# Storing later images' rows from GpSimd, scores two steps behind, and picking two experts' rows by products

## The reference

```python
x = x + mixer(_ln_c(x));  t = t + ffn(_ln_t(t))
# block 0: attention over neighbours (12 heads, dilations 1, 2, 3), then one expert of 3 per image
# block 1: Fourier mixer, then 2 experts of 8 per token with a capacity
# block 2: full attention, 12 heads of 16, relative positions, then 2 experts of 8 per token:
probs = softmax(xs @ Wg);  topv, topi = top_k(probs, 2);  cw = topv / sum(topv)
h = relu(dispatched @ W1[e] + b1[e]);  y = h @ W2[e] + b2[e]      # dispatched: tokens sorted by expert
combined = einsum('ks,ksm->sm', cw, rerouted)
# block 3: full attention as in block 2, then one expert of 3 per image
```

## Time and profile before

| | us |
|---|---|
| median of three runs | 855.84 |
| lowest and highest run | 851.66, 859.10 |
| the profiled execution | 851.86 |
| its span, first to last instruction | 850.2 |
| TensorE busy | 666.7 |
| VectorE busy | 376.5 |
| ACT busy | 302.4 |
| GpSimd busy | 202.7 |

### The profile page before, as it was taken

How to read it: one execution, slowest core, us unless ns; L and a number is a source line. 1 busy time by engine, 2 the same in 40 slices (tenths; PEclk the granted TensorE clock), 3 DMA queues, 4 the chain that set the end, 5 groups by cost and what they waited for, 6 DMA issues and landing times. The chain is left out here.

```text
span 850.2 us, 12727 instructions
## 1 busy us (share of the span) xinstructions
PE 666.7 (78%) x3982; PEld 554.7 (65%) x3982; DVE 376.5 (44%) x955; ACT 302.4 (36%) x600; POOL 202.7 (24%) x218
## 2 busy tenths in 40 slices
PE   4896755997996999939986981099995797799297
PEld 2574634695794999925665771099995366577286
DVE  4564645214445244334664745034431466575401
ACT  2343424232312444414343541044452243345222
POOL 5153440001100244421122402523344202231000
PEclk9987987698996999968898985589998689899699
DMA  3736510544106366324765304437762349660342
GB/s 100 188 94 162 140 32 22 124 118 108 31 1 167 103 160 156 52 49 114 197 168 144 93 8 135 148 89 172 184 145 32 79 148 212 169 139 2 83 111 86
DMA packets 96067, 94.93 MB, mean 112 GB/s; under 512 B 17441, under 2 KB 84020, under 8 KB 96008
## 3 DMA queue, kind: packets, MB, share of 16 engines
q1 hardware_dynamic: 85224, 80.25, 35.6%
q0 software_dynamic: 9120, 12.87, 8.6%
q10 hardware_dynamic: 1680, 1.28, 0.6%
HBM read 66.74 MB, written 27.84 MB: 111 GB/s over the span
## 5 line engine op out<-in xcount | busy, mean ns | idle before, releaser
L1925 POOL DMA_INDIRECT sum_scratch<-area,f_row_index x48 | 72.2, 1504 | 189.0 <-DVE area L1876 179.2
L843 DVE TENSOR_REDUCE neg_max<-psum 128x4 f32<-128x1024 f32 x72 | 88.0, 1222 | 65.8 <-PE psum L739 65.5
L921 POOL TENSOR_TENSOR shift<-ident,neg_max 128x256 fp32r<-128x256 f32 x96 | 69.4, 732 | 142.7 <-DVE neg_max L843 85.2
L1651 PE MATMUL psum<-w,area 128*112 128x192 f32 (+1 forms) x576 | 96.2, 326 | 0.0
L1651 PEld LDWEIGHTS psum<-w,area 128*112 128x112 f32 (+1 forms) x576 | 93.4, 183 | 0.0
L751 PE MATMUL psum<-q_parts,k_parts 128*128 128x256 f32 x288 | 84.3, 321 | 5.3 <-POOL shift L921 5.3
L739 PE MATMUL psum<-k_parts,q_parts 128*128 128x256 f32 x288 | 54.4, 316 | 37.4 <-DMA k_parts<-k_scratch 28.8
L752 PE MATMUL psum<-shift,ones_r 128*128 128x256 f32 x288 | 77.3, 297 | 0.0
L751 PEld LDWEIGHTS psum<-q_parts,k_parts 128*128 128x128 f32 x288 | 59.5, 207 | 23.3 <-issue 15.7
L739 PEld LDWEIGHTS psum<-k_parts,q_parts 128*128 128x128 f32 x288 | 43.3, 209 | 44.8 <-issue 31.2
L1745 DVE TENSOR_TENSOR q_parts<-w,q_parts 128x1536 fp32r<-128x1536 f32 x16 | 28.1, 1758 | 90.7 <-ACT q_parts L1676 90.7
(11 more groups left out here) (230 smaller groups left out, 1250.5 us busy)
## 6 DMA issues: line engine op xcount, KB each, us to landing
w<-in_f_w_dram SPq DMA_DIRECT2D x32, 576.0 KB, 4.6
w<-in_f_w_dram SPq DMA_DIRECT2D x16, 384.0 KB, 5.2
w<-in_f_w_dram SPq DMA_DIRECT2D x32, 192.0 KB, 5.8
q_parts<-q_scratch SPq DMA_DIRECT2D x32, 192.0 KB, 3.4
q_scratch<-area SPq DMA_DIRECT2D x22, 192.0 KB, 2.2
q_scratch<-area SPq DMA_DIRECT2D x44, 96.0 KB, 1.9
k_parts<-k_scratch SPq DMA_DIRECT2D x63, 64.0 KB, 3.1
q_parts<-q_scratch SPq DMA_DIRECT2D x32, 96.0 KB, 2.6
```

Of the source, the lines that this page charges most:

```text
L843: ins = dve.tensor_reduce(most, ps[:, 0:2, :].rearrange("p b (c k) -> p (b c) k", c=2), AX_X, ALU.max, negate=True)
L921: ins = nc.gpsimd.tensor_tensor(*shift_of(n, s, b))
L1651: ins = pe.matmul(ps[0:R, 6 + c // 2, D * (c % 2):D * (c % 2 + 1)], x.hidden[:, fc, R * c:R * (c + 1)], net.w2[:, b, fc, :], start=(fc == ...
L1925: pool.indirect_dma_start(net.sum_dram[:, :], bass.IndirectOffsetOnAxis(ap=row_index[0:size, b, c:c + 1], axis=0), x.y[0:size, b, c, :], N ...
```

## The change

In all three attentions the rows of images 2 and 3 are stored by another queue. `rest` lists the stores of an image. GpSimd issues two of them in each step of images 0 (for image 2) and 1 (for image 3), which are now both written out ahead of its loop; in the later two attentions the first six of 16 stay on SP, for image 2 ahead of `load_image(1)` and for image 3 between its pieces. In the first attention the tables go in fours behind pieces 1 and 3 of each image. Also in the first attention only, scores and exponentials run two steps behind (`behind = 2`), scores stand ahead of the quad's products, `finish` takes place at even steps and `store_heads` at odd ones. In f2 the rows of experts 0 and 1 aren't read back for the products: `pick_rows` multiplies the tokens, split into high and low parts by `Norm` ahead of the block, with a 128 x 384 matrix per tile of tokens that marks the slot of each token (`mark_slots`, three buffers), 32 products for an expert. The sorted rows are still stored and loaded, for the weights of all experts and the rows of experts 2 to 7. `rounds` is worked out ahead of the places, and `know_rows` stands ahead of `results` (in f1 too).

```diff
     def all_steps(eng, step, peeled=1):
...
+    behind = 2 if m.local else 1
+    rest = [(kind, half, part) for kind in (*range(kinds), KEY) for half in range(2) for part in range(2)]
+    rest_of_sync = 0 if m.local else 6
+    rest_per_step = 2
...
+            def load_image(i, between=()):
                 for piece, (first, last) in enumerate(PIECES):
                     sp.wait_ge(scored, i * HEADS + (last - HEADS))
                     load_queries(sp, i, piece)
                     load_keys(sp, i, piece)
+                    if piece % 2 == 1:
+                        for kind, half, part in between[piece // 2::2]:
+                            store(sp, kind, half, part, 3, 4, sync_written[3])
+                        if prep:
+                            start_loads(net, sp, itertools.islice(later_tables, 4), prep.loaded)
...
+            for kind, half, part in rest[0:rest_of_sync]:
+                store(sp, kind, half, part, 2, 3, sync_written[2])
+            load_image(1, rest[0:rest_of_sync])
             for i in (2, 3):
-                for kind in (*range(kinds), KEY):
-                    for half in range(2):
-                        for part in range(2):
-                            store(sp, kind, half, part, i, i + 1, rest_written[i])
-                load_image(i - 1)
-                if prep:
-                    start_loads(net, sp, prep.third[i - 2::2], prep.loaded)
-                sp.wait_ge(rest_written[i], DMA * 2 * (of_keys + 2))
-            load_image(IMGS - 1)
+                need(sp, sync_written[i], DMA * rest_of_sync)
+                sp.wait_ge(rest_written[i], DMA * (len(rest) - rest_of_sync))
+                load_image(i)
+            if prep:
+                start_loads(net, sp, later_tables, prep.loaded)
...
+                scores = not peeled or s >= behind
+                if scores and behind == 2:
+                    score(i * PAIRS + (s - behind), (s - behind) % PAIRS)
...
+                if behind == 2 and s % 2 == 0 and not isinstance(i, int):
+                    finish(i - 1, s // 2)
...
+            def store_rest(i, s):
+                at = rest_of_sync + rest_per_step * s
+                for kind, half, part in rest[at:at + rest_per_step]:
+                    store(pool, kind, half, part, i, i + 1, rest_written[i])
+
             def step(i, s):
                 shift(i, s)
                 if isinstance(i, int):
+                    store_rest(i + 2, s)
+                if isinstance(i, int) and i == 0:
                     return
                 if s in (1, 3):
                     stage_v(i, s // 2)
-                if m.local and s % 2 == 0:
+                if m.local and s % 2 == 1:
                     store_heads(i - 1, s // 2)
...
+            pool.wait_ge(high_sb, len(units))
+            pool.wait_ge(low_sb, len(units))
+            for _ in all_steps(pool, step, 2):
...
+    def split_high(self, act, q):
+        act.copy(net.experts.high[:, tiles, :], net.x_norm[:, tiles, 0:D]).then_inc(self.tokens_high, 1)
+    def split_low(self, dve, q):
+        dve.tensor_tensor(net.experts.low[:, tiles, :], net.x_norm[:, tiles, 0:D], net.experts.high[:, tiles, :], ALU.subtract)
...
+            def pick_rows(r, e):
+                for t in range(TILES):
+                    pe.wait_ge(slots_marked, START + (r * PICKED_BY_PRODUCT + e) * TILES + (t + 1))
+                    for k, size in enumerate((P, D2)):
+                        for n, part in enumerate((x.high, x.low)):
+                            ins = pe.matmul(ps[0:size, k, 0:used], part[:, t, P * k:P * k + size], x.is_slot[t % 3],
+                                            start=(t == 0 and n == 0), stop=(t == TILES - 1 and n == 1))
+                    ins.then_inc(slots_used if t < TILES - 1 else turned, 1)
...
-                if turn_next:
+                if turn_next and isinstance(e, int) and e + 1 < PICKED_BY_PRODUCT:
+                    pick_rows(r, e + 1)
+                elif turn_next:
                     turn_rows(r, e + 1, 1 - b)
...
+                step(dve.tensor_tensor(K, A, B, ALU.add))
+                step(dve.scalar_tensor_tensor(out=K, in0=counts[0], scalar=float(slots), in1=K, op0=ALU.add, op1=ALU.mult))
+
+            def mark_slots(r, e):
+                dve.wait_ge(turned, START + job(r, e))
+                for t in range(TILES):
+                    if t >= 3:
+                        dve.wait_ge(slots_used, (r * PICKED_BY_PRODUCT + e) * (TILES - 1) + (t - 2))
+                    dve.tensor_scalar(x.is_slot[t % 3], gate.places[:, 0, :], kept[:, t, e:e + 1], None,
+                                      ALU.is_equal).then_inc(slots_marked, 1)
...
                 def next_and_this(e, b):
                     low_w1(r, e + 1, 1 - b)
                     low_rows(r, e + 1)
+                    know_rows(r, e, b)
                     results(r, e, b)
-                    know_rows(r, e + 1, 1 - b)
 
                 if capacity is None:
+                    mark_slots(r, 0)
                     low_w1(r, 0, 0)
                     low_rows(r, 0)
-                know_rows(r, 0, 0)
+                    for e in range(1, PICKED_BY_PRODUCT):
+                        mark_slots(r, e)
```

96 lines of the change are left out of this document (66 added, 30 removed).

## The result

The changed kernel took 815.21 us in the median of four runs (812.35 to 818.29), the kernel before 853.82 beside it; the ratio is 0.954, with a 95% interval of 0.947 to 0.961. The forecast was 803, its range 792 to 822, 95% for faster. The median of one more measurement of the same kernel was 811.25 (ratio 0.948, 0.944 to 0.952). So the sign and the range held, and the likeliest value was 8 to 12 us too low.

The account below looks back on a forecast made before the run. No engine was taken to bound the whole; the chain is a string of stages, each with its own bound. Gains of 14.5 + 12.1 + 9.5 + 13.8 = 49.9 us from 851.86 gave 802.0, put at 803.0; range 792 to 822.

Parts of the forecast that it names:

- Part 1: First attention's image turns: SP's issuing without the stores about even with the steps; 1.5 us of lateness (0 to 4).
- Part 2: First attention, scores two steps behind: waits for POOL vanish, 2.37 us a step, 17.0 us go from 57.28.
- Rival (e): First attention: two steps behind brings nothing, 2.48 to 2.59 us a step, 806 us; counted inside the forecast's 59%.
- small term for image 0: First attention's image 0: six steps also lose the wait for the shift, about 1 us more gained.
- Part 3: POOL as new store queue: 0.55 us a store, lateness charged 1.0 us in the first attention, 0.8 in each later one.
- (c): Rival: POOL becomes the bound at 1.0 us a store, 5 + 4 + 4 us less gain, 815 us; 8%.
- (d): Rival: slower through 56 stores on POOL, at 1.8 us a store or more; about 868 us at 2.2; 3%.
- Part 4: Second and third attention: time lost at image turns goes, gaining 12.1 and 9.5 us.
- rival (a): Attentions: loads stay late through landing times, store traffic only moved; half the turns' loss stays, 822 us; 15%.
- Part 5: Second expert block: experts 0 and 1 get rows by products instead of waiting for sorted rows, gaining 13.8 us.
- picks of expert 1 5.7: Second expert block: the products that pick expert 1's rows take 5.7 us.
- rival (b): Second expert block: 16 marks delay POOL's stores by 7 us, picks all at low clock; 3 to 6 less, 808; 15%.

Follow-up runs that it names:

- e1: Changed kernel with all 30 table loads of the first attention behind image 3's loads on SP's queue; 810.65 us, ratio 0.951.
- e9: Changed kernel with 18 of 30 table loads at the start of the first attention's block, 12 behind image 3's loads; 813.92 us, ratio 0.954.
- e11: Changed kernel with 10 of 30 table loads behind the first layer norm's own loads, 20 behind image 3's loads; 807.33 us, ratio 0.946.
- e4: Changed kernel with all stores of images 2 and 3 back on SP's queue, tables in halves, as in the kernel before; 847.67 us, ratio 0.993.
- e2: Changed kernel with the first attention's scores, exponentials and finished quads one step behind instead of two; 810.93 us, ratio 0.950.
- e8: Changed kernel with the edits of e1 and e2 together: tables last and one step behind; 811.71 us, ratio 0.949.
- e5: Changed kernel measured once more, nothing edited, as base for the runs beside it; 811.25 us, ratio 0.948.
- e7: Changed kernel with GpSimd's 16 indirect stores of the second expert block begun only after TensorE picked expert 1's rows; 833.12 us (one run).
- e6: Changed kernel with five buffers of marks instead of three; 813.69 us, ratio 0.951.
- e10: e9 plus idle-time TensorE products of 128 columns in the second expert block, 60 ahead of the first picks and 32 behind; 828.65 us, ratio 0.971.
- e12: e11 plus idle-time TensorE products of 256 columns in the second expert block, 26 ahead of the first picks and 14 behind; 808.10 us, ratio 0.946.

## Why the prediction was right, and where it was off

**Part 1, SP's lateness: too small by 3 to 4 us, and the wrong allowance.** The step that failed is "It is about even ... so I add 1.5 us of lateness". The issue times were right (pieces of three in 1.25 to 1.37 us, tables 0.28 to 0.49), and so was the sum of SP's work per image, which leaves no slack. I charged it as if a queue with no slack lost little. The turns came to 45.8 us in place of the 42.8 of the sum. e1, e9 and e11 show that without the tables between pieces the turns take 41.1, within 0.8 of the 40.3 for 17 intervals at 2.37; with them 45.8 to 46.5.

**Part 2, two behind: step length right, its price left out.** An undisturbed pair takes 4.70 to 4.83 us, 2.35 to 2.42 a step. But a piece of `q_parts` and `k_parts` can be loaded only when its heads have been scored, and scoring a step later hands the loads a step (2.35 us) less before the look that needs them. I did not put that in the sum. The four corners show it: one behind 45.1 with and without the tables, two behind 45.8 to 46.5 with and 41.1 without; and with the stores on SP as well (e4) 61.05 against 57.28. That this lost step is the mechanism is argued from the order of the program; that the two edits depend on each other is shown. Rival (e), two behind brings nothing, is what the changed kernel in fact did, but not by the rival's way: it had the steps at 2.48 to 2.59 us, and they took 2.35 to 2.42. That its price, 3 us, was about the size of the miss in this stretch is luck. The small term for image 0 held: from the first maximum to (1,0) it takes 14.95 us, 15.89 before, though all of it began 0.5 later.

**The tail.** Charged 1.0 for the extra score, and that was right: from the last maximum to the last head store it takes 8.17 us before and 9.13 in the changed kernel, and with one behind 8.2 to 8.3 (e2, e8). In the changed kernel the tail grew by 2.5, in e5 by 4.3, and the rest lies behind that store. From there to the reload of the heads it takes 4.5 us before and in e4, where no table stands behind the last loads and SP has the stores, and 5.8 in all the others but e1 (8.9) and e8 (7.1), which have 30 tables there. Which of the two makes the 1.3 us no run separates; from 10 to 20 tables it does not grow. The reload with the products behind it takes 9.3 us before, 9.5 in the changed kernel and up to 11.3 in e5.

**Part 3, GpSimd.** 0.52 to 0.54 us a store against the 0.55 taken; the scores' wait for GpSimd is 0.4 us. Rivals (c) and (d) needed 1.0 and 1.8 us a store and are out.

**Part 4.** 12.1 and 8.4 us against 12.1 and 9.5; over the profiles with stores on GpSimd the means are 10.8 and 9.6. e4 loses them again, which refutes rival (a), that the loads stay late by their landing times: the same transfers, only issued elsewhere, give 54 to 58 us or 66.5 to 67.6.

**Part 5.** Gain 11.5 in the first profile and 10.2 in the mean of the eight that leave this block as it is (209.9), against 13.8. Counted from attention 2's last maximum, expert 0 began at 46.9 us where the sum had 48.9 (66.6 before): the first mark came 1.4 us sooner than forecast and the picks took 7.1 against 8.2 (7.1 to 8.5 in the others, at 0.32 us a product of the low clock and not 0.356), and TensorE then stood 2.2 us, as in the sum (3.1 in e5 and 4.0 in e9, where ACT's copy of the picked rows already came late). From expert 0 to expert 1 it was 21.6 us where the sum had 18.0. So the miss of 1.6 to expert 1's start is 3.6 less 2.0, and the 2.0 hid a part of it. The term that failed is "picks of expert 1 5.7": 9.0 us, and 6.7 to 10.7 in the other profiles. The size of the work was right, as e7 shows (5.58); what was missing is that VectorE and ACT start late behind TensorE beside GpSimd's 16 stores. I had looked at this pair of engines for the reverse, rival (b), marks that delay the stores. A mark lengthened a store by at most 0.2 us (1.14 to 1.16 for 0.97). The long `tensor_tensor` of 1.75 us is another matter, here in the changed kernel:

```profile
511.31 1.75 DVE L1821 TENSOR_TENSOR q_parts<-w,q_parts 128x1536 fp32r<-128x1536 f32 x1
511.44 2.46 POOL L2028 DMA_INDIRECT sorted_scratch<-x_norm,f_to_row  x1 [0.31 <-issue]
```

The store ends 0.84 us after the step does. In the earlier trace rows it is 0.85 us (a store of 1.42, begun 1.19 us into the step). So it is in all twelve profiles in which a store began 0.09 to 1.29 us into such a step: it ends 0.83 to 0.85 us after it. A store that began from 0.3 us ahead to 0.01 us behind the step's start took 0.97 to 0.99 as ever. By these rows the issue of a store that begins inside the step is held until the step ends. The rule weighed in the prediction (the Trainium skill, SBUF — State Buffer, Who interferes with whom) lets `tensor_scalar` lock GpSimd out for its whole length in one of its modes; the marks did not. That they ran in such a mode no row shows: they took 0.42 us for 384 columns, 1.1 ns each, as the `tensor_tensor` did. Of `tensor_tensor` with both inputs in SBUF the same section says that it contends with GpSimd's reads, and infers that it leaves descriptor writing alone; the rows show an indirect store held all the same.

**Sum.** Of the 10.9 us between 49.9 and 39.0, 5.1 lie in the first attention, 2.3 in the picks, 1.1 in attention 3, and 2.7 in a stretch that no edit touches and that no other profile repeats; the rest gave back 0.3.

## What to carry over

When a queue has about as much work as time, read for each item in it what waits for it, and move the items that nobody waits for to where the queue is empty and the transfers too; e11 did that with 10 of 30 loads, and its profile has the gain in all three stretches, while 18 of them a few microseconds later (e9) or all at the end (e1) moved a large part of the loss elsewhere. A change that works a step further behind takes, by the reading of Part 2, that step from whatever refills its buffers; count it together with the queue that does the refilling. And a hand-over between two engines that is free by itself can cost 1.4 us or more beside a run of indirect stores: keep short ping-pong chains (mark, four products, mark) out of their time.

## What the runs showed of the hardware that was not expected

- Beside a run of 16 indirect stores from GpSimd (one each 1.27 us) VectorE and ACT start late behind the TensorE products that they wait for, by 5.0 us in e6 and by 8.5 at the most (the eighth mark of e10, at 527.04 behind products that began at 517.57 to 518.20). It begins 8.5 to 9.2 us after the first store where something waits then (e7, e5), and in e7 it moved with the stores, from the marks to the relus. The cause is open.
- An indirect store whose issue begins 0.09 us or more into VectorE's 128x1536 `tensor_tensor` of 1.75 us ends 0.83 to 0.85 us after that step (12 profiles), so that it takes 1.36 to 2.51 us for 0.97.
- A float32r product of 128 columns took 0.213 us at 1.2 GHz (e10), twice what the 0.32 us for 384 columns gives by proportion.
- In e10 the granted clock (0.50, 1.2 GHz) did not rise in the 13 us of these products, though TensorE was busy 5.00 of 5.00 us; in e12, behind 26 products of 256 columns, it stood at 1.00 (2.4 GHz). The two differ in the columns, the number and the moved operand (`ones_r`, `shift`), and no run here separates these.
- Four stores that SP issues in 2.69 us took 5.45 when its tables and GpSimd's loads of constants were still under way (e9); the transfer share from 25 to 30 us was 1.05 there and 0.78 in the changed kernel. So issuing on SP took longer where the transfers were full.
